# One-hot arrays of a routing step made in one instruction per column group or in 64 small ones

## The chip, the cores and the metric

The kernel runs on one core of a Trainium2 chip. Its engines work at the same time and are held together by semaphores: TensorE (PE, with PEld for its weight loads), VectorE (DVE), ScalarE (ACT), GpSimd (POOL) and the queues that start transfers (SP for most of them). The metric is the device time of one execution in microseconds (us). The kernel before takes 781.67 us, the median of three runs (780.27 to 784.72).

## The reference

Two layers work on 2 x 1024 tokens of 256 numbers. Layer 0 is cross-attention to 77 context rows and a mixture of experts with 8 experts of which each token uses 2; layer 1 is a linear layer with a context mean and a second mixture with a hidden width of 1024. What matters here is the routing of each mixture:

```python
logits = x2 @ router_w
probs = jax.nn.softmax(logits, axis=-1)
top_p, top_e = jax.lax.top_k(probs, K)          # K = 2 of E = 8
flat_e = top_e.reshape(-1)
tok = jnp.repeat(jnp.arange(T), K)
order = jnp.argsort(flat_e)                     # entries sorted by expert
se, sp, st = (flat_e[order], flat_p[order], tok[order])
xd = x2[st]                                     # rows gathered in that order
...
out = jnp.zeros((T, Dm), x.dtype).at[st].add(y)
```

So each of the 4096 (token, choice) entries gets a place in a list sorted by expert, and the experts then work on the rows in the order of that list.

## The kernel before, in words

The tokens are in 16 tiles of 128 (NT = 16). The kernel has these stages, one after the other: attention with normalisation and the first router's logits, `route(0)`, the expert slots of the first mixture (23 slots of 256 rows, NQ = 46 tiles of places), combination with the linear layer and the second router's logits, `route(1)`, the expert slots of the second mixture (39 slots of 128 rows, NQ = 39), and the last combination. There is no scheduler: each engine has its own program, written out in order, and waits for named semaphores.

`route(layer)` exists once in the program of each engine. On VectorE it finds the two best experts of each token and, with counts from TensorE, the place of each entry in the sorted list (L993 to L1035). Most of these instructions are chained by `link`: each waits until the one before it has written. A place is split into `rr`, its low 7 bits (a row within a tile of 128), and `qq`, the number of the tile (L1039 to L1042). Both hold one value per partition for each of 32 columns n, a column being a tile of tokens and a choice. From these the kernel makes two arrays of zeros and ones in float16: `at_q`, where element (n, q) is 1 if q is the tile of the place (L1044), and `onehots`, where element (n, r) is 1 if r is the row of the place (L1048, in two halves of 16 columns). GpSimd multiplies `at_q` by the number of the token (L543, `number_tokens`). TensorE adds up 32 products of `onehots[n]` and `at_q[n]` in one PSUM bank (L1426, shown in the profile as L1240, the line of the helper): the result holds at row r of tile q the number of the token that belongs there, with its sign for the choice. VectorE makes the `index` of it (L1060 to L1063) and signals `routed`.

The order around this place is set by semaphores. `tiles_hot` lets GpSimd start its product, `places` tells TensorE that the product is there, `rows_hot` tells TensorE that a half of `onehots` is there, and `tokens_done` lets VectorE read the bank. Between the one-hot arrays and L1060, VectorE runs four small chained instructions that make the table of experts (L1052 to L1057). After `routed` GpSimd gathers the rows of the first slots with indirect DMAs (L552), TensorE transposes them (L1439), and the slots follow. SyncE's queue waits for `routed` once too (L401), and ScalarE in the first routing for `gates_ready`, which VectorE gives just behind it (L1074).

Of the kernel before, what the change touches and what calls it, by code (L numbers as in the profile page):

```python
# [6 lines left out]
F32, F16, I32, U32 = mybir.dt.float32, mybir.dt.float16, mybir.dt.int32, mybir.dt.uint32  # L7
ALU = mybir.AluOpType
# [3 lines left out]
P = 128  # L12
# [46 lines left out]
def build(nc, x, ctx_t, wq, wk, wv, scale_q, scale_k, wo, bo, rw0, w_in0, b_in0, w_out0, b_out0,  # L59
# [3 lines left out]
    NT = T // P  # L63
# [12 lines left out]
    NSLOTS = [(2 * T + E * (a * P - 1)) // (a * P) for a in TILES]  # L76
    NQS = [a * n for a, n in zip(TILES, NSLOTS)]
    LAG = 2
    WS = 64.0
    PS = 1024.0  # L80
    LN_EPS, RMS_EPS = 1e-5, 1e-6
# [5 lines left out]
    with ExitStack() as ctx:  # L87
# [5 lines left out]
        def sem(name):  # L93
            if name not in sems:
                sems[name] = ctx.enter_context(nc.semaphore(name))
            return sems[name]
# [65 lines left out]
        iota_r = sb("iota_r", [P, P], F16)  # L162
        tokens = sb("tokens", [P, NT, 2], F32)
# [36 lines left out]
        for store, src in ((wb_in, w_in0), (wb_out, w_out0)):  # L200
            v = store.rearrange("p (e s n) -> p e s n", s=2, n=per)
            g = CH // per
# [5 lines left out]
        for store, src in ((w1s, w1_t), (w2s, w2_t)):  # L208
            v = store.rearrange("p (e s n) -> p e s n", s=2, n=per)
            for e in range(E):  # L210
                for part in range(per // CH):
                    c = slice(part * CH, (part + 1) * CH)
# [64 lines left out]
        routes = [route0, route1]  # L277
        onehots = [onehot0, onehot1]
# [145 lines left out]
        def _(pool):  # L424
            g = nc.gpsimd
# [108 lines left out]
                if 0 <= s - 6 < NT and (PRE + s - 6) % 2 == 0:  # L534
                    split_lo(PRE + s - 6)

            def number_tokens(layer):

                NQ = NQS[layer]
                at_q = routes[layer][:, 128:128 + NT * NQ].bitcast(F16).rearrange("p (n q) -> p n q", q=NQ)  # L540
                num = tokens[:, :, :].rearrange("p t c -> p (t c)")[:, :, None].to_broadcast([P, 2 * NT, NQ])
                pool.wait_ge(sem("tiles_hot"), layer + 1)
                g.tensor_tensor(at_q, at_q, num, ALU.mult).then_inc(sem("places"), 1)  # L543

            def gather_rows(layer, j):

                m = moes[layer]
# [7 lines left out]
                        gathered(layer, j)[0], 16)  # L555

            def slot_rows(layer):
                number_tokens(layer)
                pool.wait_ge(sem("routed"), layer + 1)
                for b in range(2):  # L560
                    pool.wait_ge(sem(f"rows_kept{1 + 2 * layer}_{b}"), 16 * (NT // 2))
                m = moes[layer]
                for j in range(m.AHEAD):
                    gather_rows(layer, j)
                if layer == 1:
                    pool.wait_ge(sem("back_ready"), 1)
                for j in range(m.NSLOT + 3 * layer):
                    if j + m.AHEAD < m.NSLOT:
                        gather_rows(layer, j + m.AHEAD)
                    if layer == 1 and j >= 3:  # L570
                        scatter_y(j - 3)
                    if layer == 0:
                        k = PRE + A_CH + j
                        if k < NCH - LATE and k % 2 == 0:
                            split_lo(k)
                if layer == 0:
                    for b in range(m.YB):
                        pool.wait_ge(sem(f"y_kept0_{b}"), 16 * len(range(b, m.NSLOT, m.YB)))
# [214 lines left out]
        def _(dve):  # L793
            v = nc.vector
# [35 lines left out]
            y, t = k_tmp[:, 0, :], k_tmp[:, 1, :]  # L830
# [138 lines left out]
            def route(layer):  # L969
# [22 lines left out]
                for c, m in enumerate((m1, m2)):  # L992
# [6 lines left out]
                    if c == 0:  # L999
# [41 lines left out]
                link(v.tensor_copy(rr, hot[:, 0:2 * NT].bitcast(U32)))  # L1041
                link(v.tensor_copy(qq, tot[:, 0:2 * NT].bitcast(U32)))  # L1042
                at_q = r[:, 128:128 + NT * NQ].bitcast(F16).rearrange("p (n q) -> p n q", q=NQ)
                v.tensor_tensor(at_q, iota_r[:, None, 0:NQ].to_broadcast([P, 2 * NT, NQ]),  # L1044
                                qq[:, :, None].to_broadcast([P, 2 * NT, NQ]), ALU.is_equal).then_inc(sem("tiles_hot"), 1)
                for half in range(2):
                    n = slice(half * NT, (half + 1) * NT)
                    v.tensor_tensor(onehots[layer][:, n, :], iota_r[:, None, :].to_broadcast([P, NT, P]),  # L1048
                                    rr[:, n, None].to_broadcast([P, NT, P]), ALU.is_equal).then_inc(sem("rows_hot"), 1)

                ge_e = r[:, 1376:1376 + NSLOT * (E - 1)].rearrange("p (s e) -> p s e", e=E - 1)
                link(v.tensor_tensor(ge_e, iota_r[:, 0:NSLOT, None].to_broadcast([P, NSLOT, E - 1]),  # L1052
# [183 lines left out]
        def _(pe):  # L1236
            t = nc.tensor
# [174 lines left out]
            def route(layer):  # L1412
                r = routes[layer]
                hot = r[:, 5 * P:5 * P + NT * E]
                pe.wait_ge(sem("hot"), layer + 1)
                if layer == 0:
                    pe.wait_ge(sem("pt_lo"), NG * NT)
                mm(bank[7][:, 128:128 + NT * E], ones[:, :], hot, True, True)
                mm(bank[7][:, 256:256 + NT * E], before[:, :], hot, True, True).then_inc(sem("counts_done"), 1)
                NQ = NQS[layer]  # L1420
                at_q = r[:, 128:128 + NT * NQ].bitcast(F16).rearrange("p (n q) -> p n q", q=NQ)
                pe.wait_ge(sem("places"), layer + 1)
                for n in range(2 * NT):
                    if n % NT == 0:
                        pe.wait_ge(sem("rows_hot"), 2 * layer + n // NT + 1)
                    last = mm(bank[6][:, 0:NQ], onehots[layer][:, n, :], at_q[:, n, :], n == 0, n == 2 * NT - 1)  # L1426
                last.then_inc(sem("tokens_done"), 1)

# [158 lines left out]
```

## Time and profile before

| what | value |
|---|---|
| time, median of three runs | 781.67 us |
| time of the profiled execution | 779.35 us |
| its span | 777.6 us |
| busy PE / DVE / ACT / POOL | 574.8 / 569.7 / 363.6 / 457.8 us |
| mean granted clock of TensorE | 0.87 of full speed |
| route(0), from the first one-hot instruction to L1060 | 293.07 to 302.67 us |
| route(1), the same stretch | 518.76 to 528.00 us |

Times in the profile are microseconds from the start of the span. A row of the timeline has the start, the time until the end, the engine, the line, the operation, what it writes and reads, and how many instructions were merged in it. A row of the chain has the start, the length and what the program's end depended on then. The instruction's shape is partitions x elements. The buffers have names of regions: `w_region` or `slot_region` holds the arrays of the routing, `iota_r` the numbers 0 to 127, `tokens` the token numbers.

### The profile page before, as it was taken

The page shows a single profiled execution, that of the slowest core. Times are in us where ns is not written, and L with a number is a line of the kernel's source. Part 1 is how long each engine was busy: PE and PEld are TensorE (multiplying, and loading weights), DVE is VectorE, ACT ScalarE, POOL GpSimd, SP SyncE. Part 2 cuts the span into 40 slices and gives each one's busy share as a digit, 9 for nine tenths or more (in the row PEclk, how much of TensorE's full clock was granted, in tenths as well). Part 3 has the DMA queues.
Part 4 walks back from the last instruction along what each step waited for, and adds up shares of the span by engine and source line. Part 5 has one row for each costly group of instructions (what it writes and reads, how often), then busy time and mean ns, then how long its engine had stood idle before and what let it go on. Part 6 is the DMA issues. An engine that isn't in the chain of part 4 may idle for free.

```text
span 777.6 us, 17860 instructions
## 1 busy us (share of the span) xinstructions
PE 574.8 (74%) x6556; PEld 516.8 (66%) x6556; DVE 569.7 (73%) x1071; ACT 363.6 (47%) x554; POOL 457.8 (59%) x392
## 2 busy tenths in 40 slices
PE   5846889999998631787774355306999999999960
PEld 4636889988987521566653244305999999999960
DVE  3973479999999666567743687696877777777747
ACT  1754247777776432556531366731443434343320
POOL 6574478888889415777731888354355555454430
PEclk9988599999999875889978577756999999999995
DMA  8300001221222242687664232111011111112118
GB/s 280 93 4 28 28 2 42 64 69 44 61 70 69 68 122 82 179 245 234 169 190 141 83 100 84 42 54 56 29 42 56 45 54 50 50 50 49 35 53 307
DMA packets 35157, 68.50 MB, mean 88 GB/s; under 512 B 5761, under 2 KB 21890, under 8 KB 34818
## 3 DMA queue, kind: packets, MB, share of 16 engines
q1 hardware_dynamic: 25442, 42.70, 17.3%
q0 software_dynamic: 7488, 20.46, 9.5%
q10 hardware_dynamic: 2144, 4.19, 1.5%
q8 instruction: 57, 0.93, 0.5%
q14 instruction: 26, 0.21, 0.1%
HBM read 49.90 MB, written 17.43 MB: 87 GB/s over the span
## 4 chain that ended last, share of the span: by engine, by line
PE 45%; DVE 22%; POOL 8%; ACT 8%; DMA 8%; issue 8%; SPq 0%; DVEq 0%; ACTq 0%; POOLq 0%
PE banks L1240 42%; DMA slot_region<-normed_rows,index 5%; POOL wb_region L585 2%; PE banks L1439 2%; POOL w_region L467 1%; DVE x_res L1166 1%; DVE w_region L908 1%; DVE heads L900 1%; DVE w_region L913 1%; ACT w_region L691 1%; ACT w_region L624 1%; POOL slot_region L552 1%; DMA w_region<-token_y 1%; DVE w_region L1048 1%; DVE slot_region L1048 1%
## 5 line engine op out<-in xcount | busy, mean ns | idle before, releaser
L1240 PE MATMUL banks<-w_region 128*128 128x128 f16 (+5 forms) x1948 | 175.6, 252 | 31.9 <-POOL w_region L543 12.1
L1240 PEld LDWEIGHTS banks<-w_region 128*128 128x128 f16 (+1 forms) x1948 | 160.8, 126 | 42.1 <-POOL w_region L543 12.4
L1240 PE MATMUL banks<-w_region,wb_region 128*128 (+1 forms) x1000 | 121.8, 278 | 11.3 <-DMA wb_region<-wk 6.7
L594 POOL DMA_INDIRECT token_y<-slot_region,lg x39 | 65.6, 1682 | 101.1 <-DVE slot_region L1118 100.8
L1240 PEld LDWEIGHTS banks<-w_region,wb_region 128*128 128x128 f16 (+1 forms) x1000 | 101.1, 106 | 22.9 <-issue 7.8
L552 POOL DMA_INDIRECT slot_region<-normed_rows,index x85 | 95.1, 1119 | 32.3 <-issue 22.7
L1240 PE MATMUL banks<-slot_region,staging 128*128 128x128 f16 x1872 | 112.4, 221 | 0.7 <-DVE staging L1094 0.7
L751 ACT ACTIVATE wb_region<-wb_region 128x1024 f32<-128x1024 f32 x39 | 41.3, 1058 | 147.7 <-DVE wb_region L1103 147.7
L1240 PEld LDWEIGHTS banks<-slot_region,staging 128*128 128x128 f16 x1872 | 107.7, 99 | 1.0 <-issue 0.9
L1094 DVE COPY staging<-w_region 128x2048 f16 x78 | 54.4, 700 | 45.8 <-PE banks L1240 45.3
L1240 PE MATMUL banks<-wb_region,w_region 128*128 (+1 forms) x344 | 55.8, 314 | 14.4 <-ACT w_region L658 10.3
L1240 PEld LDWEIGHTS banks<-wb_region,w_region 128*128 128x128 f16 (+1 forms) x344 | 40.6, 124 | 26.7 <-ACT w_region L658 13.4
L1439 PE MATMUL banks<-ident_h,slot_region 128*128 128x128 f16 x340 | 31.6, 231 | 32.9 <-DMA slot_region<-normed_rows,index 32.6
L502 POOL TENSOR_TENSOR heads<-heads,neghalf 128x16 f32<-128x16 f32 x16 | 47.7, 2982 | 5.8 <-DVE heads L876 5.8
L1439 PEld LDWEIGHTS banks<-ident_h,slot_region 128*128 128x128 f16 x340 | 24.8, 104 | 38.3 <-DMA slot_region<-normed_rows,index 36.2
L1103 DVE SCALAR_TENSOR_TENSOR wb_region<-banks,b_s 128x1024 f32<-128x1024 f32 x39 | 47.1, 1207 | 2.0 <-PE banks L1240 2.0
L1110 DVE TENSOR_TENSOR wb_region<-wb_region 128x1024 f16<-128x1024 f32 x39 | 47.2, 1209 | 0.6 <-ACT wb_region L755 0.6
L1082 DVE COPY slot_region<-banks 128x512 f16<-128x512 f16 (+1 forms) x62 | 31.7, 512 | 21.3 <-PE banks L1439 21.3
L514 POOL TENSOR_TENSOR w_region<-w_region,heads 128x1232 f32<-128x1232 f32 x16 | 36.0, 2248 | 18.9 <-DVE heads L903 18.8
L467 POOL TENSOR_TENSOR w_region<-staging,w_region 128x1024 f16<-128x1024 f32 x15 | 32.2, 2147 | 22.3 <-ACT staging L627 22.2
L755 ACT ACTIVATE wb_region<-wb_region 128x1024 f16<-128x1024 f32 x39 | 41.2, 1057 | 1.5 <-PE banks L1240 0.3
L703 ACT ACTIVATE w_region<-banks 128x512 f16<-128x512 f32 (+1 forms) x48 | 23.4, 523 | 38.1 <-PE banks L1351 38.1
(238 smaller groups left out, 1109.8 us busy)
## 6 DMA issues: line engine op xcount, KB each, us to landing
staging<-w_t SPq DMA_DIRECT2D x24, 512.0 KB, 4.2
sorted_y<-slot_region SPq DMA_DIRECT2D x23, 256.0 KB, 5.6
w_region<-w_t SPq DMA_DIRECT2D x8, 512.0 KB, 6.0
x_res<-x SPq DMA_DIRECT2D x4, 512.0 KB, 9.5
staging<-w_in SPq DMA_DIRECT2D x4, 512.0 KB, 3.6
normed_rows<-w_region SPq DMA_DIRECT2D x16, 128.0 KB, 1.7
staging<-w_out SPq DMA_DIRECT2D x4, 512.0 KB, 3.6
normed_rows<-wb_region SPq DMA_DIRECT2D x16, 128.0 KB, 2.2
```

The costliest lines, as they stand in the source:

```text
L467: g.tensor_tensor(chunks[k][2], staged(k), chunks[k][1], ALU.subtract).then_inc(sem(f"chunk_lo{k % 2}"), 1)
L502: link(g.tensor_tensor(v, v, neghalf[:, 0:1].to_broadcast([P, NH]), ALU.pow))
L514: g.tensor_tensor(p_rows(i), p_rows(i), rs[:, :, None].to_broadcast([P, NH, L]), ALU.mult).then_inc(sem("weights_ready"), 1)
L552: g.indirect_dma_start(out=m.rows[:, j % m.RING, a, :], out_offset=None, in_=rows_dram, in_offset=bass.IndirectOffsetOnAxis(ap=index[:, q: ...
L594: g.indirect_dma_start(out=y_token, out_offset=bass.IndirectOffsetOnAxis(ap=back[:, j:j + 1], axis=0), in_=m.y[:, j % m.YB, 0, :], in_offs ...
L751: s_.activation(v, v, ACT.Gelu_apprx_tanh).then_inc(sem("gelu"), 1)
L755: s_.activation(m.hh[:, j % 2], v, ACT.Copy).then_inc(sem("h_hi"), 1)
L1094: v.tensor_copy(w_slot[:, :, half], src[:, :, half]).then_inc(sem("slot_weights"), 1)
L1103: v.scalar_tensor_tensor(out=m.g[:, j % 2], in0=hidden(m, j), scalar=1.0 / WS, in1=bias[:, :, None].to_broadcast([P, m.HC, m.SW]), op0=ALU ...
L1110: v.tensor_tensor(m.hl[:, j % 2], m.g[:, j % 2], m.hh[:, j % 2], ALU.subtract).then_inc(sem("h_lo"), 1)
L1240: return t.matmul(o, a, b, start=start, stop=stop)
L1439: last = t.transpose(cols[:, c, a * P:(a + 1) * P], m.rows[:, j % m.RING, a, c * P:(c + 1) * P], ident_h[:, :])
```

## The change

The three VectorE instructions that make `at_q` and `onehots` become 64: for each of the 32 columns one that compares `iota_r` with the column's `qq` and multiplies by the token's number, and one that compares `iota_r` with the column's `rr`. In place of arrays stretched over a whole dimension they read `qq`, `rr` and the token number as per-partition scalars. GpSimd's product and its two semaphores go. TensorE waits for `rows_hot` every 8 columns, four times in place of two.

```diff
+    HOT = 8
...
-            def number_tokens(layer):
-                NQ = NQS[layer]
-                at_q = routes[layer][:, 128:128 + NT * NQ].bitcast(F16).rearrange("p (n q) -> p n q", q=NQ)
-                num = tokens[:, :, :].rearrange("p t c -> p (t c)")[:, :, None].to_broadcast([P, 2 * NT, NQ])
-                pool.wait_ge(sem("tiles_hot"), layer + 1)
-                g.tensor_tensor(at_q, at_q, num, ALU.mult).then_inc(sem("places"), 1)
...
             def slot_rows(layer):
-                number_tokens(layer)
                 pool.wait_ge(sem("routed"), layer + 1)
...
-                v.tensor_tensor(at_q, iota_r[:, None, 0:NQ].to_broadcast([P, 2 * NT, NQ]),
-                                qq[:, :, None].to_broadcast([P, 2 * NT, NQ]), ALU.is_equal).then_inc(sem("tiles_hot"), 1)
-                for half in range(2):
-                    n = slice(half * NT, (half + 1) * NT)
-                    v.tensor_tensor(onehots[layer][:, n, :], iota_r[:, None, :].to_broadcast([P, NT, P]),
-                                    rr[:, n, None].to_broadcast([P, NT, P]), ALU.is_equal).then_inc(sem("rows_hot"), 1)
+                num = tokens[:, :, :].rearrange("p t c -> p (t c)")
+                for n in range(2 * NT):
+                    v.tensor_scalar(at_q[:, n, :], iota_r[:, 0:NQ], qq[:, n:n + 1], num[:, n:n + 1], ALU.is_equal,
+                                    ALU.mult)
+                    ins = v.tensor_scalar(onehots[layer][:, n, :], iota_r[:, :], rr[:, n:n + 1], None, ALU.is_equal)
+                    if n % HOT == HOT - 1:
+                        ins.then_inc(sem("rows_hot"), 1)
...
-                pe.wait_ge(sem("places"), layer + 1)
                 for n in range(2 * NT):
-                    if n % NT == 0:
-                        pe.wait_ge(sem("rows_hot"), 2 * layer + n // NT + 1)
+                    if n % HOT == 0:
+                        pe.wait_ge(sem("rows_hot"), (2 * NT * layer + n) // HOT + 1)
                     last = mm(bank[6][:, 0:NQ], onehots[layer][:, n, :], at_q[:, n, :], n == 0, n == 2 * NT - 1)
```

On VectorE, in `route(0)` of the kernel before (`dve_chain` is the semaphore of `link`):

```order
L1042 CAST w_region<-w_region 128x32 [waits dve_chain]
L1044 TENSOR_TENSOR w_region<-iota_r,w_region 128x1472 [waits dve_chain]
L1048 TENSOR_TENSOR w_region<-iota_r,w_region 128x2048 x2
L1052 TENSOR_TENSOR w_region<-iota_r,w_region 128x161
L1055 TENSOR_REDUCE w_region<-w_region 128x23 [waits dve_chain]
```

And in the changed kernel, the first and the last of the 32 pairs (the lines have moved by 7 or 8):

```order
L1034 CAST w_region<-w_region 128x32 [waits dve_chain]
L1038 TENSOR_SCALAR w_region<-iota_r,w_region,tokens 128x46 [waits dve_chain]
L1040 TENSOR_SCALAR w_region<-iota_r,w_region 128x128
...
L1038 TENSOR_SCALAR w_region<-iota_r,w_region,tokens 128x46
L1040 TENSOR_SCALAR w_region<-iota_r,w_region 128x128
L1045 TENSOR_TENSOR w_region<-iota_r,w_region 128x161
L1048 TENSOR_REDUCE w_region<-w_region 128x23 [waits dve_chain]
```

Three instructions of 1472 and twice 2048 elements are now 32 of 46 and 32 of 128 elements in turn. None but the first waits for anything. What follows them is as it was.

On TensorE, at the same place before (the first two rows are the counts, the others the 32 products):

```order
L1240 MATMUL banks<-w_region,ones 128x128 [waits pt_lo,hot]
L1240 MATMUL banks<-w_region,before 128x128
L1240 MATMUL banks<-w_region 128x46 [waits rows_hot,places]
L1240 MATMUL banks<-w_region 128x46 x15
L1240 MATMUL banks<-w_region 128x46 [waits rows_hot]
L1240 MATMUL banks<-w_region 128x46 x15
```

And in the changed kernel:

```order
L1233 MATMUL banks<-w_region,ones 128x128 [waits pt_lo,hot]
L1233 MATMUL banks<-w_region,before 128x128
L1233 MATMUL banks<-w_region 128x46 [waits rows_hot]
L1233 MATMUL banks<-w_region 128x46 x7
L1233 MATMUL banks<-w_region 128x46 [waits rows_hot]
L1233 MATMUL banks<-w_region 128x46 x7
L1233 MATMUL banks<-w_region 128x46 [waits rows_hot]
L1233 MATMUL banks<-w_region 128x46 x7
L1233 MATMUL banks<-w_region 128x46 [waits rows_hot]
L1233 MATMUL banks<-w_region 128x46 x7
```

The products stand in the same order; the wait for `places` is gone, and there are two more waits for `rows_hot`. On GpSimd one instruction less stands in front of the first gather of each mixture.

## Rows read from the trace of the kernel before

**Rows 1.** The page: busy engines, and the clock in 40 slices.

```profile
PE 574.8 (74%) x6556; PEld 516.8 (66%) x6556; DVE 569.7 (73%) x1071; ACT 363.6 (47%) x554; POOL 457.8 (59%) x392
PEclk9988599999999875889978577756999999999995
```

**Rows 2.** Busy time by stretch: both one-hot stretches.

```profile
core 0: us, PE busy (x) PEld busy (x) DVE busy (x) ACT busy (x) POOL busy (x), PEclk, DMA share, GB/s
...
293.10:302.70 9.60, 1.59 (x32) 1.34 (x32) 9.46 (x8) 0.00 (x0) 4.63 (x1) 0.50 0.01 2
...
518.80:528.10 9.30, 1.43 (x32) 1.20 (x32) 9.16 (x8) 0.00 (x0) 4.25 (x1) 0.50 0.00 0
```

**Rows 3.** The chain of waits, first routing and start of the slots.

```profile
294.76 6.86 DVE w_region L1048 x2
301.62 0.25 DVE w_region L1052
...
303.64 1.24 POOL slot_region L552
...
307.68 4.17 DMA slot_region<-normed_rows,index
```

**Rows 4.** The timeline, first routing.

```profile
293.07 1.69 DVE L1044 TENSOR_TENSOR w_region<-iota_r,w_region 128x1472 f16<-128x1472 f16 x1
294.68 6.94 DVE L1048 TENSOR_TENSOR w_region<-iota_r,w_region 128x2048 f16<-128x2048 f16 x2
294.84 4.63 POOL L543 TENSOR_TENSOR w_region<-w_region,tokens 128x1472 f16<-128x1472 f16 x1 [15.97 <-DVE w_region L1044]
...
301.55 0.31 DVE L1052 TENSOR_TENSOR w_region<-iota_r,w_region 128x161 f32<-128x161 f16 x1
...
301.68 0.79 PE L1240 MATMUL banks<-w_region 128*128 128x46 f16 x16 [1.35 <-DVE w_region L1048]
...
302.67 0.20 DVE L1060 TENSOR_SCALAR w_region<-banks 128x46 f32<-128x46 f32 x1
```

**Rows 5.** The timeline, second routing.

```profile
518.76 1.46 DVE L1044 TENSOR_TENSOR slot_region<-iota_r,slot_region 128x1248 f16<-128x1248 f16 x1
520.14 6.56 DVE L1048 TENSOR_TENSOR slot_region<-iota_r,slot_region 128x2048 f16<-128x2048 f16 x2
520.30 4.25 POOL L543 TENSOR_TENSOR slot_region<-slot_region,tokens 128x1248 f16<-128x1248 f16 x1 [5.04 <-DVE slot_region L1044]
...
526.62 0.43 DVE L1052 TENSOR_TENSOR slot_region<-iota_r,slot_region 128x273 f32<-128x273 f16 x1
```

**Rows 6.** L1048 alone: durations in ns (least, median, most), starts.

```profile
L1048 DVE TENSOR_TENSOR w_region<-iota_r,w_region x2: 2282/3512/4742, 294.7 to 296.9; 128x2048 f16<-128x2048 f16 x2
L1048 DVE TENSOR_TENSOR slot_region<-iota_r,slot_region x2: 2283/3321/4359, 520.1 to 522.3; 128x2048 f16<-128x2048 f16 x2
```

**Rows 7.** Groups by form on VectorE: count, busy us, mean ns, idle before.

```profile
L1094 DVE COPY staging<-w_region 128x2048 f16 x78 | 54.4, 700 | 45.8 <-PE banks L1240 45.3 <-issue 0.3
L848 DVE TENSOR_SCALAR ctx_bias<-w_region 128x256 f16<-128x256 f32 x2 | 0.6, 293 | 0.1
```

**Rows 8.** The timeline of VectorE between the routings.

```profile
458.30 0.47 DVE L1195 SCALAR_TENSOR_TENSOR x_res<-wb_region,gates,x_res 128x256 f32<-128x256 f32 x1
458.69 0.42 DVE L1199 BATCH_NORM_STATS2 st<-x_res 128x6 f32<-128x256 f32 x1
459.03 0.41 DVE L1202 BATCH_NORM_STATS2 st<-x_res 128x6 f32<-128x256 f32 x1
...
460.92 0.16 DVE L929 SCALAR_TENSOR_TENSOR lg<-banks,rbb 128x8 f32<-128x8 f32 x1
460.99 0.48 DVE L1189 SCALAR_TENSOR_TENSOR x_res<-wb_region,gates,x_res 128x256 f32<-128x256 f32 x1
```

**Rows 9.** Groups by form on ScalarE: with and without per-partition scalars.

```profile
L667 ACT ACTIVATE w_region<-x_res,rv 128x256 f32<-128x256 f32 x32 | 17.9, 589 | 7.0 <-POOL rv L481 7.0
...
L676 ACT ACTIVATE w_region<-w_region 128x256 f16<-128x256 f32 x32 | 12.1, 407 | 0.4
```

## The prediction

> **What bounds the kernel now.** I read the page first. No engine is busy all the time, the busiest being PE with 74% and DVE with 73% [rows 1], so the end is set by stages that wait for each other, and a change is worth what it does to the stage it stands in. In the slices of the clock the lowest digits, 5, include slices 16 and 27, in which the two routings lie [rows 1]. The view by stretches then shows what happens in the two places that the change touches: in 9.6 and 9.3 us PE is busy 1.6 and 1.4 us, ACT not at all, DMA at next to nothing, and DVE all but 0.14 us [rows 2]. In these two stretches the kernel is VectorE and nothing else. The chain of waits says the same: it runs through L1048 for 6.86 us, through L1052, and from there to the first gathers and their landing [rows 3]. By the code SyncE and GpSimd wait for `routed` and ScalarE for `gates_ready` in the first routing, all given behind this point. So I take each microsecond that the stretch gains or loses as one microsecond of the kernel, in both routings.
>
> The timeline shows how these stretches are made up. In the first routing L1044 starts at 293.07, L1052 at 301.55 [rows 4]: 8.48 us for the three instructions. In the second it is 518.76 to 526.62, 7.86 us [rows 5]. Together 16.34 us, and this is the number that the new instructions must beat. It holds a loss that the code doesn't show. The two halves of L1048 have the same 2048 elements, but one takes 2.28 us and the other 4.74 us, and in the second routing 2.28 and 4.36 us [rows 6]. GpSimd's product starts just behind the first half, at 294.84, and ends at 299.47; 299.47 + 2.13 us (2048 elements at 0.96 per ns) is 301.60, when the second half ends [rows 4]. In the second routing 524.55 + 2.13 = 526.68, and it ends at 526.70 [rows 5]. So the two engines took turns: GpSimd's product waited for the first half, and the second half for the product. That costs 4.74 - 2.28 = 2.46 and 4.36 - 2.28 = 2.08 us, 4.54 us in all.
>
> **The change part by part.** *GpSimd's product goes.* With it the 4.54 us of turns go, and nothing else: it is hidden behind DVE's work otherwise. TensorE loses its wait for `places`, on which only the first 16 products stand, which can start when it ends at 299.47 and last 0.8 us as the second 16 do, long before the second half of L1048 is there [rows 4]. That wait is worth nothing.
>
> *The three large instructions go.* Without the turns they would take 16.34 - 4.54 = 11.8 us in both routings.
>
> *The 64 small instructions come, twice.* Their cost is the distance from one start to the next, since an instruction that waits for nothing starts before the last one is written. Three parts make it up. First the elements. L1044 and L1048 run at one element per cycle (0.96 per ns): 2048 of them are 2133 ns of 2282 [rows 6]. A TENSOR_SCALAR from float32 in SBUF does better, 256 elements in 293 ns, which is two per cycle and about 160 ns of fixed time. A COPY with float16 on both sides does 2048 elements in 700 ns, four per cycle and about 167 ns [rows 7]. The new instructions have one stream, float16 on both sides, so I take four per cycle: 128 elements are 33 ns, 46 are 12 and 39 are 10. Second the fixed time that doesn't overlap. L1199 starts 340 ns before L1202, with 256 elements or 267 ns: 73 ns. L929, with 8 elements, starts 70 ns before L1189 [rows 8]. I take 73. Third the per-partition scalar. L1195 multiplies by a column of `gates`; it starts 390 ns before L1199, with the same 256 elements: 50 ns more than the neighbours that have no such scalar. Its duration and that of L1189, 470 to 480 ns beside 410 to 420, say the same [rows 8]. No row shows a TENSOR_SCALAR with one, nor any DVE instruction with two. The 50 ns is the nearest row and I take it for each of the two kinds, since two scalars may well be fetched together.
>
> A pair then costs (12 + 73 + 50) + (33 + 73 + 50) = 291 ns. 32 pairs are 9.3 us, in the second routing 9.2 to 9.3. Against 8.48 and 7.86 us this is +0.8 and +1.4 us, together +2.3 us with the rounding of the terms. The break-even is 16.34 / 64 = 255 ns for a pair.
>
> The bounds of the pair: below, the scalars cost nothing, 12 + 33 + 2 x 73 = 191 ns, or 12.2 us for both routings, a gain of 4.1 us. Above, elements at one per cycle as in the instructions they replace (133 + 48 ns), 73 ns each, and 50 ns for each of the three scalars: 181 + 146 + 150 = 477 ns, 30.5 us, a loss of 14.2 us. ScalarE pays more for its two scalars, 589 ns against 407 with the same 256 elements, 182 ns or 91 for each [rows 9]; for a DVE instruction it would be a far price, and I use it only to see that a second scalar need not be free.
>
> The trace shows time between starts that many small instructions pay and a large one pays once. The Trainium skill says so too: in "VectorE: DVE Perf Modes", the section on the TRN2 errata, SBUF latency is exposed between instructions, and it advises tiles of at least 512 elements, which speaks against this change. Its table there would make a fixed part of 58 cycles, an estimate of 94 and 72 ns for the two kinds, 10.6 us for both routings and a gain of 5.7 us. The rows with 73 ns and a scalar's 50 ns behind it don't bear this low price out, so I don't use it.
>
> *TensorE's products by eights.* Behind the last pair 8 products are left in place of 16, 0.4 us in place of 0.79 [rows 4]. VectorE's own four chained instructions last from 301.55 to 302.67 in any case, 1.1 us, and cover both: 0. That cover is there in either kernel; without it, it would be a gain of 0.4 us. No other engine waits behind the new waits, since TensorE has nothing else to do.
>
> *What is behind.* The gathers, the transposes and the slots start by `routed`, so they move as a block. The clock is at 0.50 in both stretches [rows 2] and PE has nothing that would raise it in the new form either. I put its effect at 0, with 1 us on either side.
>
> Sum: the profiled execution took 779.35 us for a span of 777.6. With +2.3 it would take 781.6. The median of the runs is 781.67, 2.3 us above that execution; the same sum on it gives 784.0 us.
>
> **The rivals.** *A: the scalars are free.* An instruction with 46 or 128 elements is short, and the fetch of its scalars may go on while the one before it still streams. For it speaks that the 50 ns are seen behind and in instructions of another kind, with two streams; against it that L1189 started 70 ns behind a tiny one and still took its full 480 ns [rows 8]. The pair is 191 ns and the time 781.7 - 4.1 = 777.6 us. This is the case in which the change is faster, and the skill's low price would lead there too.
>
> *B: each scalar is fetched by itself.* The compare-and-multiply has two, so the pair is 341 ns: 21.8 us against 16.34, +5.5, 787.1 us. For it speaks that ScalarE's price for two is large [rows 9], against it that nothing on DVE shows it.
>
> *C: one element per cycle.* That is the slow side by one mechanism. The streams of L1044 and L1048 are float16 and yet ran at one per cycle; if a compare with per-partition scalars has no faster way either, the pair is 181 + 146 + 100 = 427 ns with two scalars fetched together, 27.3 us, +11.0: 792.7 us. The fixed parts of a pair are 146 + 100 = 246 ns; the loss passes 3.9 us at 316 ns for a pair, so this rival decides from 70 ns for the elements of a pair, where four per cycle makes 45 and two per cycle 91. For it speaks that the replaced instructions are no evidence of speed; against it that they have two streams, one of them stretched, and that both one-stream forms in rows 7 are faster.
>
> **How the numbers follow.** Forecast (pair near 291 ns, 270 to 330 with the clock's 1 us): 48%. A: 17%. B: 17%. C: 15%. Something else, such as the turns' loss lying otherwise than I read it: 3%. The predicted time is 784.0 us. The forecast's own range is 782 to 787. The range for 8 in 10 takes in A's centre and all of B, and ends short of C: 777.3 to 791.0 us. About 0.5%, or 3.9 us, is what a measurement of this kernel can tell from no change: below 777.8 is faster, above 785.6 slower. Faster is a little over half of A with a little of the rest: 0.12. Slower is all of C, most of B and a fifth of the forecast: 0.39. The same: 0.49.
>
> **What the changed profile would show.** Right, if the distance of the first pair's start to that of L1045 is near 9.3 us in both routings, the single instructions last some 215 to 235 ns (duration is the distance and about 80 ns), GpSimd is idle there, and L1053 follows 1.1 us behind L1045's start. A would show pairs 191 ns apart, B a compare-and-multiply longer than the compare despite fewer elements by more than 25 ns, C a compare of 128 elements near 330 ns. I would be wrong in the whole if the slots' stage behind a routing changed by another amount than the routing did, as by gathers that land earlier than something else they need, or if the time moved with neither.

## The result, and the profile after

The changed kernel takes 789.47 us (median of 6 runs, 786.86 to 791.80) where the kernel before takes 781.45 us in the same comparison (6 runs). The ratio is 1.0089, with a 95% interval of 1.0064 to 1.0114: the change makes the kernel 5.0 to 8.9 us slower. The forecast was 784.0 us with a range of 777.3 to 791.0; the time lies in the range, but above the likeliest case's own 782 to 787. Of the cases, rival B (each scalar is fetched by itself, 787.1 us) comes nearest, 2.4 us below the measured median.

The first view is again the one of the two stretches, from the first one-hot instruction to just behind the reading of the bank. It answers to [rows 2]; the columns are the same.

```profile
292.90:305.80 12.90, 1.96 (x32) 1.44 (x32) 12.76 (x69) 0.00 (x0) 0.00 (x0) 0.50 0.01 2
524.80:537.90 13.10, 1.79 (x32) 1.32 (x32) 12.93 (x69) 0.00 (x0) 0.00 (x0) 0.50 0.00 1
```

GpSimd has nothing to do here any more (0.00, x0), and the granted clock is 0.50 as before. VectorE has 69 instructions in place of 8 and is busy all the time: the stretches have grown from 9.6 and 9.3 us to 12.9 and 13.1.

The timeline of the changed kernel shows the pairs (L1038 is the compare-and-multiply, L1040 the compare). These rows answer to [rows 4, 5].

```profile
292.90 0.30 DVE L1038 TENSOR_SCALAR w_region<-iota_r,w_region,tokens 128x46 f16<-128x46 f16 x1
293.11 0.25 DVE L1040 TENSOR_SCALAR w_region<-iota_r,w_region 128x128 f16<-128x128 f16 x1
293.27 0.30 DVE L1038 TENSOR_SCALAR w_region<-iota_r,w_region,tokens 128x46 f16<-128x46 f16 x1
...
304.59 0.36 DVE L1045 TENSOR_TENSOR w_region<-iota_r,w_region 128x161 f32<-128x161 f16 x1
...
304.77 0.49 PE L1233 MATMUL banks<-w_region 128*128 128x46 f16 x8 [2.44 <-DVE w_region L1040]
...
305.76 0.20 DVE L1053 TENSOR_SCALAR w_region<-banks 128x46 f32<-128x46 f32 x1
...
524.83 0.30 DVE L1038 TENSOR_SCALAR slot_region<-iota_r,slot_region,tokens 128x39 f16<-128x39 f16 x1
...
536.42 0.45 DVE L1045 TENSOR_TENSOR slot_region<-iota_r,slot_region 128x273 f32<-128x273 f16 x1
```

The first pair begins at 292.90 and the second at 293.27. Over all 32 pairs it is (304.59 - 292.90) / 32 = 365 ns a pair, and 362 ns in the second routing. From start to start the instruction with 46 elements keeps VectorE for 204 ns, the one with 128 elements for 161 (means over the row). Their durations have medians of 320 and 272 ns. That the one with fewer elements lasts longer by more than 25 ns is what the forecast named as the sign of rival B. Behind the last pair 8 products on TensorE take 0.49 us, and L1053 reads the bank 1.17 us after L1045 has begun, so the last wait is still VectorE's own.

So the stretches from the first one-hot instruction to the table of experts are 11.69 and 11.59 us, where they were 8.48 and 7.86: +3.21 and +3.73, together +6.9 us. The two profiled executions differ by more, 788.0 - 777.6 = 10.4 us. Of the other 3.5 us, 3.0 lie between the routings, from the reading of the bank to the next first one-hot instruction: 219.07 us in the changed kernel (305.76 to 524.83), 216.09 before (302.67 to 518.76). The experiments speak against the change as the cause: the same distance is 215.5 us in the version that has only the first routing changed (308.01 to 523.54), and 215.4 us (302.25 to 517.67) and 218.6 us (304.52 to 523.16) in two whose first routing is another or that of before. So this much is the scatter of single executions, and the ratio of the runs, whose interval holds 6.9 us, is the better measure.

### The profile page after: what moved, and what is told of

It reads as the page before. It is cut to its first block, busy times and chain, and to the rows that moved or that the text cites. A ratio compares the mean times of both kernels' runs of the same rounds, so it can differ in the third digit from the quotient of the medians.

```text
span 788.0 us, 17978 instructions
## 1 busy us (share of the span) xinstructions
PE 577.3 (73%) x6556; PEld 518.6 (66%) x6556; DVE 578.7 (73%) x1193; ACT 363.7 (46%) x554; POOL 446.9 (57%) x390
## 4 chain that ended last, share of the span: by engine, by line
PE 45%; DVE 23%; POOL 8%; issue 8%; DMA 8%; ACT 7%; SPq 0%; DVEq 0%; ACTq 0%; POOLq 0%
PE banks L1233 42%; DMA slot_region<-normed_rows,index 5%; POOL wb_region L577 2%; PE banks L1431 2%; DVE x_res L1159 1%; DVE w_region L900 1%; DVE heads L892 1%; DVE w_region L905 1%; ACT w_region L683 1%; POOL slot_region L545 1%; POOL w_region L468 1%; DMA w_region<-token_y 1%; POOL rv L492 1%; DVE w_region L1038 1%; ACT w_region L616 1%
## 5 line engine op out<-in xcount | busy, mean ns | idle before, releaser
L616 ACT ACTIVATE w_region<-staging 128x1024 f16<-128x1024 f32 x26 | 27.2, 1046 | 30.7 <-DVE gates L1067 20.3
```

## The experiments

### The small forms by themselves

What a pair costs decides the case, so I measured its parts alone, in one run. The kernel before got 16 groups of VectorE instructions in front of the first routing, where nothing else is on VectorE; they write scratch.

```diff
+                    for k in range(16):
+                        ins = v.tensor_scalar(o[:, 46*k:46*k + 46], iota_r[:, 0:46], 3.0, 2.0, eq, mul)
+                    link(ins)
...
+                        ins = v.tensor_scalar(o[:, 46*k:46*k + 46], iota_r[:, 0:46], s1, None, eq)
...
+                        ins = v.tensor_scalar(o[:, 46*k:46*k + 46], iota_r[:, 0:46], s1, s2, eq, mul)
```

Here s1, s2 and s3 are columns of one value per partition, s1 and s2 neighbours in `tokens`, s3 in another tile.

> The kernel before with 16 groups of VectorE instructions added in front of the first routing, where VectorE has nothing else beside it: TENSOR_SCALAR with float16 on both sides, 46, 128 and 1024 elements, with no, one or two per-partition scalars, the 128-element form with a float32 input, and a plain TENSOR_TENSOR of 128; 16 of a form (4 of 1024) without a wait between them. They write scratch; the rest is as before. What counts is the distance from start to start. Theory: each per-partition scalar is fetched by itself, about 55 to 60 ns each, and elements run at four per cycle: 46 elements 85, 140 and 200 ns with none, one and two scalars, 128 elements 106, 161 and 221 ns, 1024 elements 340, 395 and 455 ns. Rival 1: the scalars are fetched together (55 ns for one or two), and the compare-and-multiply runs its elements at one per cycle: 46 elements 140 ns with one scalar and one operation, 175 with two operations even when the second is a constant, 1024 elements 1195 ns. Rival 2: two scalars from different tiles cost more than two that are neighbours; then the group with the distant one is the only slow one.

The view by line has the durations (least, median, most, in ns) and the starts of the first and the last instruction of a group:

```profile
L998 DVE TENSOR_SCALAR w_region<-iota_r x16: 170/172/180, 282.9 to 284.2; 128x46 f16<-128x46 f16 x16
L1001 DVE TENSOR_SCALAR w_region<-iota_r,tokens x16: 234/236/242, 284.4 to 286.5; 128x46 f16<-128x46 f16 x16
L1004 DVE TENSOR_SCALAR w_region<-iota_r,tokens x16: 229/230/241, 286.8 to 288.9; 128x46 f16<-128x46 f16 x16
L1007 DVE TENSOR_SCALAR w_region<-iota_r,tokens x16: 293/295/301, 289.2 to 292.2; 128x46 f16<-128x46 f16 x16
L1010 DVE TENSOR_SCALAR w_region<-iota_r,tokens,neghalf x16: 290/292/299, 292.6 to 295.6; 128x46 f16<-128x46 f16 x16
...
L1016 DVE TENSOR_SCALAR w_region<-iota_r,tokens x16: 245/246/254, 297.7 to 300.1; 128x128 f16<-128x128 f16 x16
```

The chain of waits has the length of each group:

```profile
282.94 1.41 DVE w_region L998 x16
284.38 2.38 DVE w_region L1001 x16
286.78 2.38 DVE w_region L1004 x16
289.19 3.35 DVE w_region L1007 x16
292.57 3.35 DVE w_region L1010 x16
295.94 1.73 DVE w_region L1013 x16
297.70 2.70 DVE w_region L1016 x16
...
303.15 3.67 DVE w_region L1022 x16
...
310.53 1.44 DVE w_region L1028 x4
312.00 1.69 DVE w_region L1031 x4
313.71 1.92 DVE w_region L1034 x4
```

A group of 16 is 15 distances and one duration, so the distance with 46 elements and no scalar (L998) is (1.41 - 0.17) / 15 = 83 ns. With one scalar (L1001) it is 143, with one scalar and a constant as the second operation (L1004) 143, with two scalars (L1007) 204, and with the second from another tile (L1010) 204 as well. With 128 elements the distances are 103 (L1013), 163 (L1016) and 224 ns (L1022). With 1024 elements there are only four of a form, and the starts in the trace give 337, 398 and 458 ns (L1028, L1031, L1034).

Each scalar costs 60 ns, the second as much as the first, and neither the second operation nor the place of the scalar costs anything. From 46 to 1024 elements without a scalar it is 255 ns for 978 elements, 3.8 for a ns: four times the rate of L1044 and L1048 before, where 2048 elements take 825 ns more than 1248 (2282 and 1457 ns), which is called one per cycle here. What is left is 70 ns per instruction. The theory holds, and both rivals fall. The pair is 204 + 163 = 367 ns, and the kernel had 365. The same compare with a float32 input of 128 elements and one scalar is 196 ns from start to start, 33 more than from float16, which is two per cycle.

### One routing at a time

In two kernels only one routing is changed.

```diff
+                if layer == 0:
+                    for n in range(2 * NT):
+                        v.tensor_scalar(at_q[:, n, :], iota_r[:, 0:NQ], qq[:, n:n + 1], num[:, n:n + 1], ...)
+                        ins = v.tensor_scalar(onehots[layer][:, n, :], iota_r[:, :], rr[:, n:n + 1], None, ALU.is_equal)
...
+                else:
                     v.tensor_tensor(at_q, ...)
```

> The first routing as changed (64 small instructions, no product on GpSimd), the second as before. Theory: what a routing's stretch loses, the kernel loses, one for one. In the changed kernel the first stretch grew from 8.48 to 11.69 us, so the time is 3.2 us above before, 784.7 us. Rival: part of the 8.0 us between the two kernels arises behind the routings (the stretches alone account for 6.9), in the gathers or the slots of the first mixture; then this kernel takes 1 us or more on top, 785.7 us or above.

> The second routing as changed, the first as before. Theory: its stretch grew from 7.86 to 11.59 us, so the time is 3.7 us above before, 785.2 us, and the two single changes add up to the whole one, 6.9 us. Rival: the start of the last mixture's slots absorbs or adds something (gathers, granted clock); then the sum of the two single changes is not the 8.0 us of the whole within the intervals.

The first routing alone gives a ratio of 1.0048 (1.0013 to 1.0083), +3.8 us on a median of 784.7 for the kernel before in this comparison; the second alone 1.0034 (0.9993 to 1.0076), +2.7 us. The stretches in their profiles are, in us from the first one-hot instruction to the table of experts, 11.69 and 7.86 with the first changed, 8.48 and 11.58 with the second: each changes by itself and leaves the other as it was. The two ratios add up to +6.5 us; the stretches say +6.9. This agrees with one for one, but the intervals are 5.5 and 6.5 us wide, and that of the second holds no change at all. The rival, 1 us or more from behind the routings, is not excluded by the runs. No profile shows it: between the routings the two kernels have 215.5 us (308.01 to 523.54) and 218.6 us (304.52 to 523.16), and the longer one is that in which nothing ahead of this part was changed. From the second reading of the bank to the end it is 252.2 us and 253.8 us, and 249.6 before and 250.2 in the changed kernel. That part too varies by some 4 us where nothing in it differs: it is 252.2 us in the next version.

### The product on VectorE

To see what the product on GpSimd had cost, I left the large instructions and moved only the product.

```diff
-                g.tensor_tensor(at_q, at_q, num, ALU.mult).then_inc(sem("places"), 1)
+                link(v.tensor_tensor(at_q, iota_r[:, None, 0:NQ].to_broadcast([P, 2 * NT, NQ]),
+                                     qq[:, :, None].to_broadcast([P, 2 * NT, NQ]), ALU.is_equal))
+                v.tensor_tensor(at_q, at_q, num, ALU.mult).then_inc(sem("places"), 1)
```

> The kernel before with its large instructions, but the product with the token numbers made by VectorE in one instruction in front of L1048, none by GpSimd. Theory of the turns: without GpSimd's two-input product both halves of L1048 take 2.28 us; the stretch is 1.61 + 1.6 + 2 x 2.2 = 7.7 us in the first routing (8.48 before) and 1.39 + 1.4 + 4.4 = 7.2 in the second (7.86), together 1.5 us less, 780 us. Rival: the second half is slow for a reason of its own (its place in memory, TensorE reading the first half beside it); then it stays at 4.4 to 4.7 us, the stretches are 10.1 and 9.4 us, and the time is 3 us above before.

The large one-hot instruction in this kernel, to be held against [rows 6]:

```profile
L1041 DVE TENSOR_TENSOR w_region<-iota_r,w_region x2: 2284/2284/2284, 296.7 to 298.9; 128x2048 f16<-128x2048 f16 x2
L1041 DVE TENSOR_TENSOR slot_region<-iota_r,slot_region x2: 2284/2284/2284, 520.5 to 522.7; 128x2048 f16<-128x2048 f16 x2
```

Both halves take 2284 ns, in both routings, though TensorE reads the first half beside the second as before. The rival falls. The turns are gone with the product, and they were 4.5 us. The stretches are 7.74 us (293.37 to 301.11) and 7.27 (517.67 to 524.94), 1.3 us less than before where 1.5 was expected. The ratio is 0.9975 (0.9946 to 1.0003), and the runs can't tell this from nothing.

### The product back on GpSimd, with small compares

The other way round: the changed kernel with the multiplication taken out of the small instructions and given back to GpSimd.

```diff
-                    v.tensor_scalar(at_q[:, n, :], iota_r[:, 0:NQ], qq[:, n:n + 1], num[:, n:n + 1], ALU.is_equal, ALU.mult)
+                    ins = v.tensor_scalar(at_q[:, n, :], iota_r[:, 0:NQ], qq[:, n:n + 1], None, ALU.is_equal)
+                ins.then_inc(sem("tiles_hot"), 1)
```

> The changed kernel with one part undone: the small compares for at_q have one scalar and come first, 32 in a row, GpSimd multiplies all of it by the token numbers again, and the 32 small compares for onehots run beside it. Theory A, from the small forms measured alone (143 and 164 ns from start to start) and if an instruction with one input doesn't take turns with GpSimd: 32 x 0.143 + 32 x 0.164 = 9.8 us against 11.7, so 1.9 and 1.8 us less than the changed kernel, if the product (some 2.5 us alone) ends before the compares. Theory B: the four-per-cycle form takes turns with GpSimd's two-input product as the large TENSOR_TENSOR did; then the compares wait some 2.1 to 2.5 us for it in each routing and the stretches are 12.0 to 12.3 us, as long as the changed kernel's or longer, and GpSimd's product spans more than 2.5 us.

```profile
L1049 DVE TENSOR_SCALAR w_region<-iota_r,w_region x32: 241/245/2722, 300.1 to 307.6; 128x128 f16<-128x128 f16 x32
L1049 DVE TENSOR_SCALAR slot_region<-iota_r,slot_region x32: 241/243/2324, 530.1 to 537.2; 128x128 f16<-128x128 f16 x32
...
L544 POOL TENSOR_TENSOR w_region<-w_region,tokens x1: 2657/2657/2657, 300.3 to 300.3; 128x1472 f16<-128x1472 f16 x1
L544 POOL TENSOR_TENSOR slot_region<-slot_region,tokens x1: 2274/2274/2274, 530.2 to 530.2; 128x1248 f16<-128x1248 f16 x1
```

Of the 32 compares 31 take about 245 ns and one takes 2722 ns, as long as GpSimd's product of 2657 ns lasts, and 2324 beside 2274 ns in the second routing. It is the second compare each time: it starts within 15 ns of the product. So a TENSOR_SCALAR with a single input, at four elements per cycle, waits for GpSimd just as the large TENSOR_TENSOR did. Theory B holds. The stretches are 12.22 and 11.77 us (B had 12.0 to 12.3 for each, A 9.8), longer than the changed kernel's 11.69 and 11.59, and the ratio is 1.0084 (1.0053 to 1.0115). The second scalar is saved in each routing (32 x 60 ns = 1.9 us) and paid again as a wait.

The Trainium skill has the condition: "GPSIMD Engine Reference", section "Specifications", says that GpSimd's SBUF interfaces are shared with VectorE and contended by VectorE instructions in a 2-port mode or with two SBUF inputs. By that rule the form of before, with two SBUF inputs, has to take turns, and the trace agrees: 2.46 us. The new form has one SBUF input, so it falls under the rule only if it runs in a 2-port mode; the trace, with a wait of about 2.5 us, fits that, but shows no mode.

### Columns innermost

L1044 and L1048 ran at one element per cycle although `iota_r` and what they write have 2 bytes. Each has a second input that is stretched in its innermost dimension, where its step is 0. That input, `qq` or `rr`, is also float32 in both kernels: the views name the first input's type alone. I turned the arrays round and made `qq`, `rr` and the token numbers float16, so this edit changes two things at once.

```diff
-        tokens = sb("tokens", [P, NT, 2], F32)
+        tokens = sb("tokens", [P, NT, 2], F16)
...
+        grids = [carve(W1R, 57344, [P, NT], F16)[0], carve(WBR, 18432, [P, NT], F16)[0]]
...
-                rr, qq = (r[:, k:k + 2 * NT] for k in (1280, 1312))
+                rr, qq = (r[:, k:k + NT].bitcast(F16) for k in (1280, 1312))
...
+                for half in range(2):
+                    ins = v.tensor_tensor(at_q[:, half], grid[:, 0:NQ, :], qq[:, None, n].to_broadcast([P, NQ, NT]), ALU.is_equal)
...
+                    v.tensor_tensor(at_q[:, half], at_q[:, half], num[:, None, n].to_broadcast([P, NQ, NT]), ALU.mult)
...
+                    v.tensor_tensor(onehots[layer][:, half], grid, rr[:, None, n].to_broadcast([P, P, NT]), ALU.is_equal)
```

> The arrays are laid out with the 16 columns of a half innermost, so that every stream is 2-byte with step 1: a constant grid (128 rows x 16 columns, made once per layer by GpSimd while it has nothing to do) is compared with qq and rr in float16, stretched only over the outer dimension; the product is on VectorE in the same form; TensorE reads its operands with a step of 16 elements. Six large instructions in place of 64. Theory: one element per cycle in L1044 and L1048 was due to a stretched innermost dimension, and two per cycle is to be had: 2 x (383 + 73) + 2 x (383 + 73) + 2 x (1067 + 73) ns = 4.1 us in the first routing against 8.48, and 3.9 against 7.86, so about 8.3 us less than before, 773 us. Rival 1: a VectorE instruction with two inputs runs at one per cycle here whatever the layout; then it is 7.7 and 7.2 us, 780 us. Rival 2: TensorE pays for the step in its weight loads; its 16 products behind the second half took 0.8 us and have 1.1 us of cover, so a load four times as long (0.2 us and more each) would give back 2 us or more per routing, 777 us.

The timeline of the first routing:

```profile
294.07 0.99 DVE L1046 TENSOR_TENSOR w_region<-w_region 128x736 f16<-128x736 f16 x2
295.10 1.00 DVE L1051 TENSOR_TENSOR w_region<-w_region,tokens 128x736 f16<-128x736 f16 x2
296.01 2.35 DVE L1055 TENSOR_TENSOR w_region<-w_region 128x2048 f16<-128x2048 f16 x2
297.28 2.95 PEld L1247 LDWEIGHTS banks<-w_region 128*128 128x128 f16 x32 [9.13 <-DVE w_region L1055]
297.28 3.15 PE L1247 MATMUL banks<-w_region 128*128 128x46 f16 x32 [8.84 <-DVE w_region L1055]
298.28 0.32 DVE L1059 TENSOR_TENSOR w_region<-iota_r,w_region 128x161 f32<-128x161 f16 x1
...
300.55 0.21 DVE L1067 TENSOR_SCALAR w_region<-banks 128x46 f32<-128x46 f32 x1 [1.17 <-PE banks L1247]
```

VectorE needs 4.21 us (294.07 to 298.28) where it needed 8.48, and 3.98 for 7.86 in the second routing: two elements per cycle, and rival 1 falls. The Trainium skill states the same rate ("VectorE: DVE Perf Modes", the perf-mode tier table: a `tensor_tensor` on bf16 in SBUF runs at most at 2x, with 1224 ns for 2048 elements), and the trace agrees, with 1220 ns for each L1055. That the stretch was the cause, as the theory had it, needs the next version, in which one compare has float16 throughout and keeps the stretch. Rival 2 is true as well: the 32 products now take 3.15 us, one starting 93 ns behind the other where it was 39, and VectorE waits 1.17 us for them at L1067, in the second routing 0.51 us. The ratio is 0.9946 (0.9916 to 0.9976), 4.2 us faster than before.

### Which operand TensorE pays for

Here only the one-hot rows, TensorE's weights, are read with a step (the edit is shown against the version with halves); `at_q` is laid out as before, and is made by a compare and a product on VectorE, now from float16 values alone.

```diff
-                    last = mm(bank[6][:, 0:NQ], onehots[layer][:, n // NT, :, n % NT], at_q[:, n // NT, :, n % NT],
+                    last = mm(bank[6][:, 0:NQ], onehots[layer][:, n // NT, :, n % NT], at_q[:, n, :],
```

> As the version with halves, but at_q as before, with the tiles innermost, in one large compare and one large product on VectorE; only the one-hot rows, TensorE's weights, are read with a step of 16 elements. Theory: the longer products come from the weight load with a step, so they stay near 98 ns each in the first routing. Rival: they come from the moving operand at_q with its step; then they fall back to 50 ns.

```profile
295.59 1.69 DVE L1044 TENSOR_TENSOR w_region<-iota_r,w_region 128x1472 f16<-128x1472 f16 x1
...
300.20 2.32 PE L1241 MATMUL banks<-w_region 128*128 128x46 f16 x32 [10.23 <-DVE w_region L1049]
```

The row L1044 settles the question of the section above. It has float16 in both inputs and in the output, `qq` is still stretched in the innermost dimension, and it takes the same 1.69 us as before. So float16 alone doesn't give two per cycle; the layout is needed. Whether the layout alone would do, with `qq` and `rr` in float32, wasn't tried.

The row of the products can't be divided by 32, since TensorE waits some 0.12 us between the halves, and the last product has its own length in it. The distances have to be taken within a half. Narrow windows of the three traces give them: two rows for this version, two for the one with both operands turned, and two for the kernel before, each time the first routing and then the second.

```profile
300.41 0.80 PE L1241 MATMUL banks<-w_region 128*128 128x46 f16 x10
524.77 0.84 PE L1241 MATMUL banks<-slot_region 128*128 128x39 f16 x11
297.76 0.91 PE L1247 MATMUL banks<-w_region 128*128 128x46 f16 x8
522.76 0.83 PE L1247 MATMUL banks<-slot_region 128*128 128x39 f16 x8 [12.31 <-DVE slot_region L1055]
301.73 0.56 PE L1240 MATMUL banks<-w_region 128*128 128x46 f16 x10
526.76 0.52 PE L1240 MATMUL banks<-slot_region 128*128 128x39 f16 x10 [1.44 <-DVE slot_region L1048]
```

Each row is its distances and the last product's own 0.23, 0.27 or 0.21 us. That makes 62 ns from start to start with the weights alone at a step, in both routings; 91 and 81 ns with both operands (93 and 80 over all 32 products); and 39 and 34 ns before. The 98, 86, 50 and 45 ns in the expectations are whole rows divided by their count. Neither theory nor rival was right: the weights' step alone costs 23 ns in the first routing.

The two steps needn't add up. With both, the distance goes with the moving columns (93 / 46 = 2.0 and 80 / 39 = 2.1 ns for each), and with the weights alone it is 62 ns for 46 columns and for 39. That fits two loads side by side of which the slower sets the pace. The moving operand with a step by itself wasn't run, so this is argued and not shown. (This version has one run, 778.7 us; its profile is what counts here.)

### Blocks of eight

The wait at the end of the version with halves (sixteen columns to a part) has a cure, since TensorE can begin earlier if the parts have eight.

```diff
+                for k, n in enumerate(parts):
+                    v.tensor_tensor(at_q[:, k], at_q[:, k], num[:, None, n].to_broadcast([P, NQ, HOT]), ALU.mult)
+                    v.tensor_tensor(onehots[layer][:, k], grid, rr[:, None, n].to_broadcast([P, P, HOT]),
+                                    ALU.is_equal).then_inc(sem("rows_hot"), 1)
```

> The layout with the columns innermost in four blocks of 8 columns, product and one-hot rows of a block one behind the other, a signal to TensorE after each. In the version with halves VectorE was done in 4.21 and 3.98 us, but the bank was read 1.17 and 0.51 us later than VectorE could, since 32 products took 3.15 and 2.75 us (98 and 86 ns each, 50 and 45 before). Theory: 8 products behind the last block are 0.8 us, under the 1.1 us of the table of experts, so the wait goes; the smaller instructions cost 6 x 73 ns more; from the first instruction to the bank's reading 4.6 + 1.1 = 5.7 us in the first routing (9.60 before, 6.48 with halves) and 5.6 in the second (9.24, 5.84); 7.5 us less than before. Rival: a step of 8 elements leaves the rate of two per cycle, or TensorE's products are slower beside VectorE's instructions than alone; then the stretches are as with halves or longer.

```profile
295.16 1.13 DVE L1047 TENSOR_TENSOR w_region<-w_region 128x368 f16<-128x368 f16 x4
296.32 0.35 DVE L1051 TENSOR_TENSOR w_region<-w_region,tokens 128x368 f16<-128x368 f16 x1
296.59 0.68 DVE L1052 TENSOR_TENSOR w_region<-w_region 128x1024 f16<-128x1024 f16 x1
...
297.33 3.49 PE L1244 MATMUL banks<-w_region 128*128 128x46 f16 x32 [7.80 <-DVE w_region L1052]
...
299.78 0.31 DVE L1056 TENSOR_TENSOR w_region<-iota_r,w_region 128x161 f32<-128x161 f16 x1
...
300.93 0.20 DVE L1064 TENSOR_SCALAR w_region<-banks 128x46 f32<-128x46 f32 x1
```

L1064 has no wait any more, as expected. From the first instruction to the reading of the bank it is 5.77 us in either routing (295.16 to 300.93 and 519.92 to 525.69), where it was 9.60 and 9.24 before and 12.86 and 12.98 in the changed kernel. That is 7.3 us less than before. The ratio is 0.9907 (0.9880 to 0.9934), also 7.3 us, at a median of 775.4 us against 781.7. This version is faster than the kernel before, and so than the changed one, which was slower.

## Why the prediction came out as it did

*The stretch is the kernel.* Right, as far as the runs can tell. In these kernels VectorE fills the stretches, and where a version moved them by much, the interval of its ratio holds that number: +6.9 us (5.0 to 8.9), -7.3 us (-9.4 to -5.2), and just about -6.5 us for the version with halves, with the wait for TensorE counted (-6.6 to -1.9). That nothing behind the routings changes by itself is shown by profiles only as far as their scatter of 4 us allows.

*The turns with GpSimd are worth 4.54 us.* Right, in size too: both halves fell to 2284 ns when the product left. That the wait for `places` was worth nothing was not tried by itself; no row speaks against it.

*The three large instructions without the turns are 11.8 us.* Right: with the product on VectorE they are 7.74 + 7.27 less two products of 1.61 and 1.37 us, 12.0 us.

*The 64 small ones.* This is the step that failed, in one term, and the case of 784.0 us, to which I gave 48%, failed with it. Elements at four per cycle (12 and 33 ns) were right. The fixed time between starts was 70 ns and not 73. The scalar was taken as 50 ns for each of the two kinds, "since two scalars may well be fetched together". They aren't: 60 ns for each, three in a pair, 181 ns where I had 100. The pair is 45 + 140 + 181 = 366 ns and not 291, and 64 of them are 23.4 us and not 18.6; the kernel's two stretches had 23.3. Of the 81 ns too few for the scalars, 20 are the two first ones, at 60 and not 50 ns, and the other 60 the second one. The low price that the prediction quotes and sets aside, 10.6 us for both routings, was indeed too low by 12.7 us, and nearly all of it, 64 x 181 ns = 11.6 us, is the scalars. Rival B had the mechanism and, with 50 ns each, 341 ns.

*TensorE by eights* was worth 0, as forecast, under the same cover. *The clock* was at 0.50 in both stretches, before and after.

*Rival C's reason* was misread. The prediction says that the streams of L1044 and L1048 are float16 and yet ran at one per cycle. The second of their streams is float32, so they were no evidence on float16 alone; the compare of the version with the rows alone turned is, at 1.69 us for 1472 elements. C itself did not come: the new instructions run at four per cycle.

*The chances.* The 17% for B were too few. The trace of before had a hint that I set aside as a far price, the 182 ns that two scalars cost on ScalarE [rows 9], and nothing in it spoke for two scalars in one fetch. The range held the time because it reached over B, not because the forecast's sum was right: 789.5 us is 1.5 us inside its end. With the measured growth of the stretches the sum would have been 781.67 + 6.9 = 788.6 us; the 0.9 us that are left are within the interval of the ratio.

## What to carry to other kernels

In these kernels a TENSOR_SCALAR on VectorE that waits for nothing keeps the engine for 70 ns, 60 ns for each per-partition scalar and its elements at the rate of its form. A large instruction of N elements at one per cycle is replaced with profit by k small ones only where their fixed parts together are less than what the higher rate saves, and here 64 fixed parts of 160 ns on average, 10.2 us, stood against the 8.48 us that the three large ones took in all. Before cutting a stretched compare into columns, ask whether the stretched dimension can be an outer one and all its inputs float16: that gave two per cycle with few instructions, and was the better way (0.9907 of the time before, in blocks of eight). And a product given to GpSimd beside VectorE's work is no gain if VectorE waits for it: look for one instruction in a group that takes longer by just the length of GpSimd's.

## What the runs showed that I had not expected

- The second per-partition scalar costs as much as the first, 60 ns, be it the neighbour of the first or in another tile, and a second operation with a constant costs nothing.
- One instruction with a single input and 2-byte values, at four elements per cycle, waited for the whole of GpSimd's product (2324 ns beside 2274); the others in the row didn't pay anything.
- At a granted clock of 0.50, products on TensorE of 128x128 weights and 46 columns follow each other by 39 ns, by 62 ns with the weights at a step of 16 elements, and by 93 ns with both operands at that step. With both, the distance goes with the number of columns; with the weights alone it doesn't.
- A compare with float16 in every place and one input stretched in its innermost dimension still ran at one element per cycle (1472 in 1.69 us).
- In the changed kernel's first routing the durations of the pairs grow along the row, the compare-and-multiply from 295 to 335 ns, while the distance between starts stays at 365 ns; in the second routing they grow by 17 ns only. What this is stays open; it moves the table of experts by 0.05 us.
